# Keys of even and odd heads in one buffer, score matmuls on 64 rows

## The reference, cut to what matters

```python
q = _apply_rope_full(x @ wq.T); k = _apply_rope_full(x @ wk.T); v = x @ wv.T     # each to [B, 16, 512, 8]
scores = jnp.einsum('bhqd,bhkd->bhqk', q, k) / math.sqrt(Dh)
scores = scores + _alibi_slopes(H)[None, :, None, None] * rel[None, None]        # rel = key pos - query pos
scores = jnp.where(causal[None, None], jnp.float32(-1000000000.0), scores)
attn = jax.nn.softmax(scores, axis=-1)
out = jnp.einsum('bhqk,bhkd->bhqd', attn, v)
return out.transpose(0, 2, 1, 3).reshape(B, S, D) @ out_w.T + out_b
```

## Time and profile before

| | |
|---|---|
| median of 3 runs | 1578.22 us (1575.39 to 1587.37) |
| time of the profiled execution | 1580.4 us |
| its span, first to last instruction | 1578.6 us |
| mean granted TensorE clock | 0.921 |
| PE busy | 1250.7 us (79%) |
| DVE busy | 1038.2 us (66%) |
| ACT busy | 603.1 us (38%) |
| POOL busy | 254.3 us (16%) |

### The profile page before, as it was taken

The page is one execution under the profiler, slowest core; times in us unless marked ns, Lnnn a source line. Parts: engine busy times, 40 slices in busy tenths (PEclk is TensorE's granted clock), DMA queues, the critical chain, the costliest instruction groups (busy, mean ns, idle before and its releaser), DMA issues.

```text
span 1578.6 us, 16492 instructions
## 1 busy us (share of the span) xinstructions
PE 1250.7 (79%) x5768; PEld 754.0 (48%) x5768; DVE 1038.2 (66%) x1997; ACT 603.1 (38%) x992; POOL 254.3 (16%) x205
## 2 busy tenths in 40 slices
PE   0998767799899465769969967678999984657798
PEld 0676433467666122226636753335766641222465
DVE  5656737355666897986646666464565759979764
ACT  5443342444322454432215424344433243454222
POOL 1001000000010363541000010000001014636210
PEclk9999898999999788789979989899999996979899
DMA  6102121000000000000001030300000000000000
GB/s 236 34 21 61 35 60 38 2 1 0 1 0 1 0 1 0 0 0 1 14 29 54 1 94 3 94 3 2 0 1 1 1 0 0 0 0 0 1 7 14
DMA packets 23543, 32.05 MB, mean 20 GB/s; under 512 B 3008, under 2 KB 19168, under 8 KB 22880
## 3 DMA queue, kind: packets, MB, share of 16 engines
q1 hardware_dynamic: 23456, 30.94, 6.7%
HBM read 23.40 MB, written 8.06 MB: 20 GB/s over the span
## 4 chain that ended last, share of the span: by engine, by line
PE 58%; DVE 23%; issue 7%; DMA 6%; ACT 5%; SPq 1%; POOL 1%; DVEq 0%; POOLq 0%; ACTq 0%
PE bank L1221 11%; PE bank L1223 10%; PE bank L1222 10%; PE bank L1383 7%; DVE n_h L1188 5%; DVE a_mx L1126 3%; PE bank L1294 3%; PE bank L1230 3%; DVE bank L1180 3%; DMA X<-in_x_dram 2%; PE bank L1440 2%; PE bank L1480 2%; PE bank L1348 2%; DMA a_k<-stack_dram 2%; PE bank L1421 2%
## 5 line engine op out<-in xcount | busy, mean ns | idle before, releaser
L991 DVE SCALAR_TENSOR_TENSOR f_hl<-bank,f_hh 128x512 fp32r<-128x512 f32 x192 | 131.8, 689 | 128.8 <-ACT f_hh L695 127.9
L695 ACT ACTIVATE f_hh<-bank 128x512 fp32r<-128x512 f32 x192 | 114.8, 598 | 207.0 <-PE bank L1294 206.6
L623 POOL TENSOR_TENSOR n_hc<-n_h,n_cs 128x512 f32<-128x512 f32 x128 | 160.6, 1272 | 127.7 <-DVE n_h L1188 79.1
L749 ACT ACTIVATE m_sl<-bank 128x512 f32<-128x512 f32 x144 | 85.9, 598 | 233.2 <-PE bank L1223 232.8
L1221 PE MATMUL bank<-xT_h,mw_h 128*128 128x512 f32 x288 | 162.7, 565 | 5.4 <-DVEq L433 4.3
L570 POOL TENSOR_TENSOR small<-small,half 128x4 f32<-128x4 f32 x24 | 24.3, 1013 | 829.5 <-DVE small L894 829.0
L1530 PE MATMUL bank<-n_hc,ident 128*128 128x512 f32 x256 | 145.8, 690 | 11.0 <-POOL n_hc L623 10.3
L1051 DVE TENSOR_TENSOR m_t<-m_sl,bank 128x512 f32<-128x512 f32 x128 | 87.8, 686 | 99.2 <-PE bank L1223 85.1
L1188 DVE TENSOR_TENSOR_SCAN n_h<-n_da,bank 128x512 f32<-128x512 f32 x128 | 149.5, 1203 | 5.0 <-POOL n_hc L623 4.9
L825 ACT ACTIVATE n_da<-n_dt,amat 128x512 f32<-128x512 f32 x128 | 91.7, 721 | 144.1 <-DVE n_h L1188 124.3
L1383 PE MATMUL bank<-m_h,mw 128*128 128x512 f32 x288 | 145.4, 593 | 0.0
(11 more groups left out here) (241 smaller groups left out, 2488.7 us busy)
## 6 DMA issues: line engine op xcount, KB each, us to landing
w_stage<-in_mw_dram SPq DMA_DIRECT2D x16, 256.0 KB, 2.7
a_q<-stack_dram SPq DMA_DIRECT2D x8, 512.0 KB, 6.2
a_k<-stack_dram SPq DMA_DIRECT2D x16, 256.0 KB, 7.7
stage_fw<-in_fw_dram SPq DMA_DIRECT2D x2, 1536.0 KB, 9.9
stack_dram<-R SPq DMA_DIRECT2D x16, 192.0 KB, 2.8
stack_dram<-R SPq DMA_DIRECT2D x16, 128.0 KB, 2.5
stage_b<-in_bias_dram SPq DMA_DIRECT2D x1, 1728.0 KB, 10.1
X<-in_x_dram SPq DMA_DIRECT2D x5, 256.0 KB, 2.8
```

The costliest lines, as they stand in the source:

```text
L623: n_hcs.by(nc.gpsimd.tensor_tensor(n_hc[:, m, :], n_h[:, m, :], n_cs[:, n // 2 % 2, :], ALU.mult))
L695: f_hi.by(act.activation(f_h[0][:, i % 4, :], bank[:, i % 3, :], ACT.Relu))
L991: f_lo.by(V.scalar_tensor_tensor(f_h[1][:, i % 4, :], bank[:, i % 3, :], 0.0, f_h[0][:, i % 4, :].bitcast(F32), ALU.max, ALU.subtract))
```

## The change

- `a_k` becomes [128, 8 pairs, 512], laid out as `a_q`. The 8 KB per partition that it gives up are taken by a tensor that nothing uses (`w_stage_home`), so that the tiles behind it keep their addresses.
- The two zero fills, the semaphore counts for them and TensorE's wait go. The fill of the values' spare columns stays.
- Keys are loaded with one DMA to a half instead of two.
- Score matmuls of both passes read 64 partitions (`head`): 0 to 63 for an even head, 64 to 127 for an odd one. The mask matmuls still take 128 rows.
- Query tile 0 is now two slots of 2 heads, so a quad has 12 slots instead of 11. A slot of two heads takes heads of one parity (0 and 2, or 1 and 3). The jobs ahead of the steps become 23.
- In a step of the second pass the two score matmuls come first, then the two mask matmuls.

```diff
-SLOTS_4 = [(0, 0, 4)] + [(qt, h, n) for qt, n in ((1, 2), (2, 1), (3, 1)) for h in range(0, 4, n)]
+SLOTS_4 = [(qt, h, 2) for qt in (0, 1) for h in (0, 1)] + [(qt, h, 1) for qt in (2, 3) for h in range(4)]
...
-        a_k = sb("a_k", [P, HEADS, T], BF16, s)
+        a_k = sb("a_k", [P, HEADS // 2, T], BF16, s)
+        sb("w_stage_home", [P, HEADS // 2, T], BF16, s)
...
+        def head(rows, h):
+            at = 64 * (h % 2)
+            return rows[at:at + 64, h // 2, :]
...
-                            for odd in range(2):
-                                a_ldk[n].by(sp.dma_start(a_k[64 * odd:64 * odd + 64, 8 * n + odd:8 * n + 8:2],
-                                                         stack_dram[1, odd][:, pairs]))
+                            a_ldk[n].by(sp.dma_start(a_k[:, pairs], stack_dram[1].rearrange("o r h t -> (o r) h t")[:, pairs]))
...
-                            for odd in (1, 0):
-                                other = a_k[64 * (1 - odd):64 * (1 - odd) + 64, odd::2]
-                                a_fill.by(nc.gpsimd.memset(other.bitcast(F32), 0.0))
-                                pool.wait_ge(a_fill.sem, a_fill.at(0, 1 - odd))
...
-                    a_m1.by(V.tensor_reduce(a_mx[:, quad, qt, h0:h0 + nh], src, AX_X, ALU.max, negate=True))
+                    a_m1.by(V.tensor_reduce(a_mx[:, quad, qt, h0:h0 + 2 * nh - 1:2], src, AX_X, ALU.max, negate=True))
...
-                pe.wait_ge(a_fill.sem, a_fill.at(0, 1))
...
-                            b = 2 * (s_ % 2) + n
-                            mm(bank[:, b, 0:w], a_k[:, h, kt * P:(kt + 1) * P], a_q[:, h // 2, kt * P:T],
-                               start=True, stop=False)
-                            ins = mm(bank[:, b, 0:P], identb, mask_kq, start=False, stop=True)
+                            mm(bank[:, 2 * (s_ % 2) + n, 0:w], head(a_k, h)[:, kt * P:(kt + 1) * P],
+                               head(a_q, h)[:, kt * P:T], start=True, stop=False)
+                        for n in range(2):
+                            ins = mm(bank[:, 2 * (s_ % 2) + n, 0:P], identb, mask_kq, start=False, stop=True)
...
-                        h = 4 * quad + h0 + c
-                        mm(bank[:, b, c * w:(c + 1) * w], a_q[:, h // 2, qt * P:(qt + 1) * P], a_k[:, h, 0:w],
+                        h = 4 * quad + h0 + 2 * c
+                        mm(bank[:, b, c * w:(c + 1) * w], head(a_q, h)[:, qt * P:(qt + 1) * P], head(a_k, h)[:, 0:w],
                            start=True, stop=False)
```

More of the change, by code:

```diff
@@ L363, in program @@
         a_res = sig("a_res", "mha", 4)
-        a_fill = sig("a_fill", "pair", 3)
+        a_fill = sig("a_fill", "pair", 1)
         a_vok = sig("a_vok", "mha", 1)
@@ L367, in program @@
         a_ldq = [sig(f"a_ldq_{n}", "mha", 1, 16) for n in range(2)]
-        a_ldk = [sig(f"a_ldk_{n}", "mha", 2, 16) for n in range(2)]
+        a_ldk = [sig(f"a_ldk_{n}", "mha", 1, 16) for n in range(2)]
         a_rld = sig("a_rld", "pair", 1, 16)
@@ L593, in _ @@
                     if kind == "mha":
-                        if k % 2 == 0:
-                            for odd in (1, 0):
-                                other = a_k[64 * (1 - odd):64 * (1 - odd) + 64, odd::2]
-                                a_fill.by(nc.gpsimd.memset(other.bitcast(F32), 0.0))
-                                pool.wait_ge(a_fill.sem, a_fill.at(0, 1 - odd))
                         prologue(u + 1, "guess")
@@ L1436, in mha @@
                             pe.wait_ge(a_vok.sem, a_vok.at(k, 0))
-                            pe.wait_ge(a_fill.sem, a_fill.at(0, 2))
+                            pe.wait_ge(a_fill.sem, a_fill.at(0, 0))
                         for c in range(4):
@@ L1456, in rows_of_half @@
                 pe.wait_ge(a_ldq[n].sem, a_ldq[n].at(k, 0))
-                pe.wait_ge(a_ldk[n].sem, a_ldk[n].at(k, 1))
+                pe.wait_ge(a_ldk[n].sem, a_ldk[n].at(k, 0))
             def bank_free(k, i):
```

## The result

The changed kernel is slower: a median of 1669.49 us (1657.83 to 1675.97, 6 runs) against 1579.05 us (6 runs), a ratio of 1.056 with a 95% interval of 1.051 to 1.061. The forecast was 1612 us with a range up to 1650, so the direction was right and the size too small by more than half. The profiled execution has a span of 1674.1 us, 95.5 us more than before, and a mean granted clock of 0.847 against 0.921.

What follows compares the result with a forecast made beforehand. VectorE was taken to pace the jobs ahead of the steps, TensorE to be nearest its limit in steps with slots. Per attention unit 2.3 + 6 + 0.7 - 0.7 = 8.3 us, 33 for four: 1612 us, range 1566 to 1650.

Steps and rivals of the forecast that it cites:

- The price of a switch: TensorE changing between 64-row and 128-row tiling: 0.12 us each, 177 switches a unit.
- Rivals 1 and 2: 1: row switches cost little, halves overlap, 1567 to 1569, chance 0.25. 2: a switch costs 0.265 us, 1700, 0.15 with rival 3.
- The overlap of the two halves: In a step, two score matmuls on different row halves run together, saving 4.3 us of TensorE a unit.
- Rival 4: The halves do not overlap, 4.3 us a unit come back: 1628 us; upper part of the forecast's own 0.60.
- Part B: An attention unit's steps with slots between them: +9.1 us on TensorE, about half its 6 us of waits filled, so +6.
- the turns and column visits: Turns and column-tile visits on TensorE in Part B: 3 us on top of 17.0 us of columns.
- rival 3: Gaps lower TensorE's clock: at 0.70 in Part B +7 us a unit, 1640; at 0.87, 1622; chance 0.15 with rival 2.
- Part A: The jobs ahead of the steps in an attention unit, 17.1 us, paced by VectorE: +2.3 us.
- Part C: An attention unit's steps without slots, 25.9 or 23.4 us: switches +2.4, overlap -1.7, so +0.7 us.
- The load: Loading queries and keys at a unit's start: larger pieces of a_k gain up to 1.8 us, taken as -0.7.
- Slots, zero fill: 23 jobs instead of 22 change nothing; dropping GpSimd's 3.66 us fill, twice, gains nothing, as TensorE did not wait for it.

Runs made afterwards that it cites:

- rows128_switch: The kernel before, scores on 128 rows, with a 64-row stand-in matmul in place of each mask (causal mask missing): 1725.13 us, ratio 1.090.
- steps_in_turn: The changed kernel, but in a second-pass step each score matmul is followed by its own mask, as before: 1749.93 us, ratio 1.105.
- key_layout: The kernel before with the zero-padded key buffer ordered by parity, then pair, so key loads land in 4 KB runs: 1579.12 us, ratio 0.999.
- slots12: The kernel before with only the regrouping of slots, 12 to a quad, all matmuls on 128 rows: 1577.46 us, ratio 0.999.
- rows64_noswitch: The changed kernel with a 64-row stand-in matmul in place of each mask (causal mask missing): 1568.94 us, ratio 0.992.
- masks_on_halves: The changed kernel with each causal mask added by two 64-row matmuls on the head's own half; computes the reference: 1570.06 us, ratio 0.993.
- slot_halves: masks_on_halves with the 128-row masks put back in the steps only: 1620.30 us, ratio 1.024.
- pass2_64: The kernel before with only the second pass's steps as in the changed kernel (two 64-row scores, then two 128-row masks): 1585.02 us, ratio 1.002.
- warm_start: The changed kernel with 22 unread matmuls of 384 columns put ahead of the first slot, during the load: 1677.06 us, ratio 1.061.

## Why the prediction was right or wrong

- **The price of a switch: right.** The forecast took 0.12 us from the column switches. The row switches measure 0.11 us: in both directions, at either clock in the changed kernel, and in `rows128_switch`. Rivals 1 and 2 fall with it. The Trainium skill (TensorEngine Tiling (Array Packing), Key Properties) says that a change of the tiling mode drains the engine. The trace agrees with that for rows too, as far as a gap of 0.11 us at each change can show it.
- **The overlap of the two halves: right.** Two score matmuls of a step last as long as one, and `steps_in_turn` gives the price of its loss in B within 0.1 us. Rival 4 falls.
- **Part B: the step that failed.** The sum let part B stream at full clock and had "Part B's clock stays above 0.9" among its signs. It was 0.50 in all four units. At half clock the forecast's own terms nearly give the measured time: 17.0 - 2.5 = 14.5 us of columns become 29, the turns and column visits, 3 us in the forecast, are some 4 with the turns at half clock (an estimate), and 97 switches of 0.11 us are 10.7: 43.7 of 45.24 us. (The columns were summed with 32 slot matmuls and the switches with 34, which is 0.7 us of the rest.) So +6 became +17.5 us: the low clock adds 14.5 us of columns, and the 3 us of waits that the forecast had left vanish in it, 11.5 us beyond the forecast. The text named this case as rival 3, but with a clock of 0.70 in B, the value of part A, and shared a chance of 0.15 with rival 2. That was the mistake: 0.70 is a mean of stretches at both levels, and the stream of B stayed at the lower one throughout.
- **Part A: too small.** Forecast +2.3 us, measured +3.5 (16.0 to 19.6), and 3.5 to 4.4 in the four units. It was costed at half clock for 60% of the time and ran so all of it. By the working of the forecast that is 1.9 quads x 2.2 = 4.2 us.
- **Part C: too small.** Forecast +0.7, measured +4.3 and +3.7 in the first two units: the low clock of B lasts into it (0.72 and 0.82 against 0.87 and 1.00).
- **The load: right in kind, small in size.** Forecast -0.7 us a unit. It was 6.1 us instead of 7.9 in the first unit and 6.1 instead of 8.3 in the third; the second and fourth gained 1.1 and 2.4. The bound for run length was up to 1.8 us, a figure that the prediction does not derive, and `key_layout` shows 1.4 us of it.
- **Slots, zero fill: right.** `slots12` at 0.999; L890 at 0.17 us.

Over the execution the load gives back about 7 us, A costs 15 and B and C together 87: 95 us, the growth of the span. The forecast had 36 for A, B and C. Nearly all of the rest goes with the lower clock. The direction came out as forecast, but most of the loss came by a path that the sum did not hold.

The switches and the rows were taken apart in runs. `rows64_noswitch` and `masks_on_halves` keep the half-used rows without switches, and the loss is gone. `rows128_switch` has full-row scores with switches, and the loss is there. `slot_halves` against `pass2_64` shows a lower clock with slots on 64 rows at one number of switches. Not shown is whether these are two causes or one, less work of the array in a microsecond, to which a gap and an empty half would both add.

The Trainium skill (TensorE: Matmul & The Clock Gate, A second HAM failure mode: psum-queue depth-cycling) describes a stream with small idle gaps between groups of matmuls whose clock swings between its two levels. The trace agrees in that small gaps go with a lost clock. It differs in that the clock did not swing in B: with 0.11 us gaps it stayed at 1.2 GHz for 45 us. What stays open is why B of one kernel has 0.50 in one unit and 0.83 in another (`slot_halves`, `rows128_switch`). The windows show only that the units differ in when the clock rises within B, if it does. No run here tells what decides that.

## What to carry to other kernels

- In this kernel matmuls on half of the rows paid only where their neighbours used the same tiling. Count the changes of tiling, take about 0.11 us for each, and if a full-array matmul must stand between two of them, ask first whether it can be written as two on the halves: here that turned 5.6% slower into 0.7% faster.
- When a change puts gaps into a busy TensorE stream, do the sum twice, at 2.4 and at 1.2 GHz. Here the profile of before did not tell which of them holds after, and the clock was most of the loss in part B. A mean clock between the two, taken from another part, is not the case to cost.
- Group what shares a tiling. The same matmuls in the order score, score, mask, mask instead of score, mask, score, mask are worth about 80 us in the changed kernel.

## What the runs showed of the hardware that I had not expected

- The clock can stand at 1.2 GHz through a stretch in which TensorE is never idle for longer than a switch: 45.03 of 45.24 us busy at 0.50.
- It depends on rows as well: with nearly the same busy time of 12.3 and 12.7 us in part A, full rows (the kernel before) gave 0.71 and half rows (`rows64_noswitch`) 0.50. Where a unit entered at 2.4 GHz (`warm_start`), the clock fell after 5.1 us.
- A switch between 64 and 128 rows costs the same time at both clocks, 0.11 us, so it does not scale with the array's clock.
- Loads whose destination lies in runs of 4 KB instead of 1 KB were 1.4 us of some 8 shorter for 1 MB.
- Beside the second of GpSimd's two fills of zeros (1.80 us each) a small VectorE operation took 1.73 us instead of 0.17 and a copy of 128x512 1.65 instead of 0.69. Both are short in the changed kernel, which has no such fill. Three kinds of VectorE operations beside the first fill kept their times, so it is not every operation. No cost shows here: the chain behind the small one ended at 160.84, before the load at 161.0.
